# Adaptive-norm network of two layers on one core: the barrier between layer 0 and the attention is taken out and the first head starts among the last batch's experts

## The reference, cut to what matters

```python
# layer 0, for each batch: linear attention (16 heads of 8) + MLP on a modulated norm, then experts
h = _layernorm(x) * (1 + ca) + sa;  x = x + ga * L0_attn(h)
x = x + gb * L0_ffn(x modulated by cb, sb)
# layer 1, attention:
xn = layer_norm(_layernorm(x) * (1 + ca) + sa)
q, k, v = heads(xn @ Wq), heads(xn @ Wk), heads(xn @ Wv)
att = einsum('bhid,bhjd->bhij', q, k) / 8 + slope[h] * -|i - j|
p = softmax(att);  x = x + ga * ((p @ v) @ Wo)
```

## Time and profile before

| | |
|---|---|
| runs | 2463.85 us median of 3 (2462.29 to 2464.60) |
| profiled execution | 2467.89 us, span 2466.0 us |
| granted TensorE clock, mean | 0.954 of full |
| busy | PE 93%, DVE 71%, POOL 56%, ACT 52% |
| the chain that ended last | PE 86%, DVE 6%, issue 3%, POOL 2% |

### The profile page before, as it was taken

How to read it: one execution, slowest core, us unless ns; L and a number is a source line. 1 busy time by engine, 2 the same in 40 slices (tenths; PEclk the granted TensorE clock), 3 DMA queues, 4 the chain that set the end, 5 groups by cost and what they waited for, 6 DMA issues and landing times.

```text
span 2466.0 us, 39735 instructions
## 1 busy us (share of the span) xinstructions
PE 2296.2 (93%) x10653; PEld 1363.7 (55%) x10654; DVE 1740.9 (71%) x4461; ACT 1285.7 (52%) x1712; POOL 1385.0 (56%) x751
## 2 busy tenths in 40 slices
PE   4989898599999999999999999999999997969995
PEld 2566565356565655555555555555556553437663
DVE  5687785477777777777777777877787864744444
ACT  1223322266666666666666666666666662314442
POOL 2121120177676768676767777777767684743221
PEclk7999898599999999999999999999999997989998
DMA  7001202100000000000000000000000002111114
GB/s 266 1 6 74 80 1 79 31 14 10 15 11 13 18 15 11 13 12 13 21 11 12 13 14 10 13 20 14 10 15 11 13 20 113 38 39 45 43 42 126
DMA packets 71231, 81.41 MB, mean 33 GB/s; under 512 B 18324, under 2 KB 56980, under 8 KB 71000
## 3 DMA queue, kind: packets, MB, share of 16 engines
q1 hardware_dynamic: 66808, 71.58, 9.2%
q0 software_dynamic: 4352, 8.99, 1.1%
HBM read 49.97 MB, written 32.66 MB: 34 GB/s over the span
## 4 chain that ended last, share of the span: by engine, by line
PE 86%; DVE 6%; issue 3%; POOL 2%; SPq 1%; DMA 1%; ACT 1%; POOLq 0%; DVEq 0%; ACTq 0%
PE P L1774 18%; PE P L1738 12%; PE P L1759 9%; PE P L1760 9%; PE P L1725 5%; PE P L1596 3%; PE P L1969 3%; PE P L1973 3%; PE P L1610 3%; PE P L1992 3%; PE P L1781 2%; PE P L1792 2%; PE P L1707 2%; PE P L1743 1%; PE P L1982 1%
## 5 line engine op out<-in xcount | busy, mean ns | idle before, releaser
L1393 ACT ACTIVATE big<-P 128x1024 f32<-128x1024 f32 x512 | 511.9, 1020 | 188.4 <-PE P L1760 84.5
L998 DVE CUSTOM_DVE_ANT_0 big<-P,near 128x512 f32<-128x512 f32 x512 | 349.0, 682 | 231.4 <-PE P L1738 231.2
L1774 PE MATMUL P<-big,V 128*64 128x512 f32 x2048 | 481.3, 602 | 0.0
L601 POOL TENSOR_TENSOR spair<-spair,big 128x1024 f32<-128x1024 f32 x192 | 456.9, 2380 | 13.2
L601 POOL TENSOR_TENSOR opair<-opair,big 128x1024 f32<-128x1024 f32 x192 | 456.6, 2378 | 13.8 <-ACT big L1393 0.6
L1738 PE MATMUL P<-Ka,Qa 96*128 96x512 f32 x1024 | 451.8, 463 | 4.8 <-DVE mhalf L998 3.3
L1001 DVE TENSOR_REDUCE mhalf<-P 128x1 f32<-128x512 f32 x512 | 349.2, 682 | 85.9 <-PE P L1738 75.9
L1759 PE MATMUL P<-Qa,Ka 97*128 97x512 f32 x1024 | 408.4, 399 | 0.5 <-ACT big L1393 0.5
L1760 PE MATMUL P<-Qb,Kb 128*128 128x512 f32 x1024 | 406.5, 397 | 0.0
L1738 PEld LDWEIGHTS P<-Ka,Qa 96*128 96x128 f32 x1024 | 185.9, 191 | 224.4 <-issue 118.6
L588 POOL TENSOR_TENSOR big<-big,sinv 128x512 f32<-128x512 f32 x64 | 81.8, 1279 | 378.5 <-DVE sinv L973 378.5
(11 more groups left out here) (288 smaller groups left out, 3483.8 us busy)
## 6 DMA issues: line engine op xcount, KB each, us to landing
slots<-later SPq DMA_DIRECT2D x4, 4224.0 KB, 13.8
Ka<-auxrows SPq DMA_DIRECT2D x66, 128.0 KB, 2.2
big<-in_wex SPq DMA_DIRECT2D x8, 768.0 KB, 9.0
xt<-slots SPq DMA_DIRECT2D x76, 66.0 KB, 1.8
wqk<-in_whead SPq DMA_DIRECT2D x66, 64.0 KB, 1.8
near<-in_aux SPq DMA_DIRECT2D x66, 64.0 KB, 1.8
big<-yrows SPq DMA_DIRECT2D x8, 512.0 KB, 7.2
hT<-hkeep SPq DMA_DIRECT2D x5, 512.0 KB, 3.8
```

The source lines that it names most:

```text
L601: pool.tensor_tensor(psum8[s][:, :], psum8[s][:, :], pfull[:, j % RING, :], ALU.add).then_inc(S["p_added"], 1)
L998: dve.tensor_tensor_reduce(scratch, P[:, 6 + i, :], near[s][:, left:left + HALF], -1.0, 3.0e38, ALU.add, ALU.min, mhalf[:, i, t:t + 1]).th ...
L1393: act.activation(pfull[:, j, :], banks(2 * (j % 2)), ACT.Exp, scale=DH1 ** -0.5).then_inc(S["exp_done"], 1)
L1774: mm = pe.matmul(P[64 * i:64 * i + 64, 4, :], V1[:, j, s, :], half(pfull[:, j, :], i), start=(j == 0), stop=(j == T - 1))
```

## The change

The barrier between layer 0 and the attention is gone (`meet(8)` and one `end_batch` on each engine), and the code of both stages is in one semaphore epoch. The parts:

- SP issues the loads for heads 0 and 1 before layer 0. After `hkeep[2]` is written it waits until it has landed and loads `hTc` from `hkeep[0]`. After the last `up` of batch 3 it loads `hT` from `hkeep[0]`.
- In batch 3, PE projects q and k of head 0 from `hTc`, half 0 before the experts (`early_qk(0, 0, 6)`), half 1 after `down(2)`, and issues the maxima of head 0 in single matmuls after the downs of u = 5 to 17 (`early_max`). ACT and DVE split and reduce them among their GELUs and gates. Three maxima, head 1's projection and the turn follow the last `down`.
- The c part of batch 3 stands beside head 0's scores: `c_residual`, the moments, `c_first`, `c_second` and `c_third` (the three parts of `c_norms`) between DVE's biases. It uses `big[0]`, `big[1]` and `spair` as buffers. Its transposes come after `weigh(5)`.
- The maxima of head 1 no longer stand beside head 0's scores; they come after the c part's copies.
- Fillers: 3 or 2, and 2, before the two halves of the turn of `o0`; 6 for 2 before `turn("b0")` from batch 1 on; 4 new ones between its halves; 5 for 4 after it.
- `half_stats` of `c0`, half 1, moves ahead of DVE's wait for the exponential of q, in batches 1 to 3.

```diff
+            for b in range(B):          # SP
+                sp.dma_start(part, over(empty, [128, quarter, chunk])).then_inc(G["filled"], 16)
+                if b == B - 1:
+                    sp.wait_ge(S["up_mm"], EACH["up_mm"] * B)
+                    sp.dma_start(hT[:, :], hkeep[0]).then_inc(S["hT_in"], 16)
+                    sp.wait_ge(S["hT_in"], 32)
+                    sp.sem_inc(S["h_ok"], 2)
+                sp.wait_ge(E["c_kept"], NHALF * (b + 1))
+                sp.dma_start(hkeep[b], kept[b]).then_inc(G["h_kept"], 16)
+                if b == B - 2:
+                    sp.wait_ge(G["h_kept"], 16 * B)
+                    sp.dma_start(hTc, hkeep[0]).then_inc(S["hT_in"], 16)
             sp.wait_ge(G["h_kept"], 16 * B + 16)
...
+                if b > 0:               # DVE, between q0_min and the wait for q0_exp
+                    half_stats(f"c0{b - 1}", 1, tok(xs[:, b - 1, :]))
...
+                if b == B - 1:          # DVE, after the router
+                    q_low(0, 0, 0, 6)
+                    k_low(0, 0, 0, 6)
...
+                    elif u == 4:        # DVE, in the experts of batch 3
+                        q_low(0, 0, 1, 7)
+                        k_low(0, 0, 1, 7)
+                    elif u >= 6:
+                        early_max(u - 6)
+            for k in range(CH0 * NHALF - 6, T * NHALF):
+                early_max(k)
+            max_both(0)
+            c_residual(B - 1)
+            q_low(1, 1, 0)
+            k_low(1, 1, 0)
+            bias(0, 0, 0)
+            bias(0, 0, 1)
+            c_moments(B - 1, 0)
+            q_low(1, 1, 1)
+            k_low(1, 1, 1)
+            bias(0, 0, 2)
+            c_moments(B - 1, 1)
+            bias(0, 0, 3)
+            c_first(B - 1)
+            bias(0, 0, 4)
+            bias(0, 0, 5)
+            c_second(B - 1)
+            bias(0, 0, 6)
+            c_third(B - 1)
+            bias(0, 0, 7)
...
+                    if b == B - 1:      # ACT, in the experts of batch 3
+                        if u == 4:
+                            q_high(0, 0, 1, 7)
+                            k_high(0, 0, 1, 7)
+                        elif u == 8:
+                            q_again(0, 0)
+                        elif u == 10:
+                            k_again(0, 0)
...
+                if t == TPH and between:    # PE, turn
+                        keep_busy(4, between)
+                    keep_busy(4, 3 if i == 0 and b > 0 else 2)
-                keep_busy(2, 10 if b == 0 else 2)
+                keep_busy(2, 10 if b == 0 else 6)
-                turn(f"b0{b}", 2)
-                keep_busy(4, 4)
+                turn(f"b0{b}", 2, between=4)
+                keep_busy(4, 5)
...
+                if b == B - 1:          # PE, after zero(1)
+                    pe.wait_ge(E["c_kept"], NHALF * b)
+                    early_qk(0, 0, 6)
...
+            for k in range(EARLY, T * NHALF):   # PE, after close(1)
+                early_max(k)
+            early_qk(1, 0, 5)
+            turn_max(0)
+            pe.wait_ge(S["xb_done"], EACH["xb_done"] * B)
+            scores(0, 0, 0)
+            scores(0, 0, 1)
+            early_qk(1, 1, 5)
+            scores(0, 0, 2)
+            project_v(0, 0)
+            scores(0, 0, 3)
+            scores(0, 0, 4)
+            project_v(0, 1)
+            scores(0, 0, 5)
+            scores(0, 0, 6)
+            scores(0, 0, 7)
+            for j in range(T - 2):
+                weigh(0, 0, 0, j)
+            turn(f"c1{B - 1}", 6, xcs[B - 1])
+            pe.wait_ge(E["c_kept"], NHALF * B)
             for t in range(T):
                 for i in range(NHALF):
+                    max_half(1, 1, t, i)
+                if t == 1:
+                    project_qk(0, 2, 0)
+                if t == 4:
+                    project_qk(0, 2, 1)
+            weigh(0, 0, 0, T - 2)
+            weigh(0, 0, 0, T - 1)
+            turn_max(1)
```

More of the change, by code:

```diff
@@ L408, in _ @@
             sp.sem_inc(S["mod_in"], 1)
[L409 to L414, removed]
             def load_qk(g, s):
@@ L578, in _ @@
                     scale(b + 1, wdowns, wdown[:, :, :], 1, "wdown_scaled")
+            add_head(0, 0, False, range(1, 2))
             inverse_root(f"c0{B - 1}")
+            add_head(0, 0, False, range(2, 3))
             inverse_root(f"c1{B - 1}")
[L581 to L604, removed]
+            add_head(0, 0, False, range(3, T))
+            pool.wait_ge(G["h_kept"], 16 * B + 16)
+            add_head(1, 1)
             def first_pairs(b, behind):
@@ L1072, in _ @@
+            max_both(1)
             head(0, 1, behind=1)
@@ L1316, in c_copies @@
                     act.wait_ge(S["turned"], NHALF * TR_TAGS[f"c1{b}"] + i + 1)
-                    act.activation(half(hTc, i), P[:, 6 + i, :], ACT.Identity, bias=vecs[:, 5 + FC:6 + FC], scale=vecs[:, 4 + FC:5 + FC]).then_inc(E["c_kept"], 1)
+                    act.activation(half(kept[b], i), P[:, 6 + i, :], ACT.Identity, bias=vecs[:, 5 + FC:6 + FC], scale=vecs[:, 4 + FC:5 + FC]).then_inc(E["c_kept"], 1)
             act.wait_ge(G["set_done"], NSET)
@@ new lines, in _ @@
+            q_high(1, 1, 0)
+            k_high(1, 1, 0)
+            maxima(0, 0)
+            exps(0, 0)
+            exps(0, 1)
+            q_high(1, 1, 1)
+            k_high(1, 1, 1)
+            exps(0, 2)
+            exps(0, 3)
+            values(0, 0)
+            q_again(1, 1)
+            exps(0, 4)
+            values(0, 1)
+            exps(0, 5)
+            exps(0, 6)
+            exps(0, 7)
+            c_copies(B - 1)
+            q_high(0, 2, 0)
+            k_high(0, 2, 0)
@@ L1454, in _ @@
+            k_again(1, 1)
+            q_high(0, 2, 1)
+            k_high(0, 2, 1)
+            maxima(1, 1)
+            q_again(0, 2)
             head(0, 1, behind=1)
@@ new lines, in down @@
+            def down(b, u):
+                if u < NHALF:
+                    pe.wait_ge(S["up_act"], EACH["up_act"] * b + u + 1)
+                else:
+                    pe.wait_ge(S["up_gated"], EACH["up_gated"] * b + u - NHALF + 1)
+                f = A[:, (0 if u < NHALF else 2) + (u % 4) // 2, (u % 2) * HALF:(u % 2 + 1) * HALF]
+                for t in range(TPH):
+                    mm = pe.matmul(bank_t(0, u % 2 * TPH + t), tile(f, t), wdowns[:, u // NHALF, :],
+                                   start=False, stop=False)
+                mm.then_inc(S["downb_mm"], 1)
```

554 lines of the change are left out of this document (293 added, 261 removed).

## The result

The kernel after the change takes 2436.19 us, median of four runs (2431.65 to 2437.33), for 2464.22 (2462.29 to 2465.82) before: a ratio of 0.9884, 95% interval 0.9869 to 0.9899, so 28 us less where 33 were forecast. The time lies in the range. The profiled execution has 2437.33 us for 2467.89, which is 30.6 less; it is the slowest of its four runs.

What follows compares the result with a forecast made beforehand. TensorE bounds attention heads and experts; time lies at the boundary and in half-clock stretches. Boundary net 20.5, statistics 2.4, fillers 8.7 and 1.4 sum to 33.0 us saved: 2434.9 profiled, 2431 forecast, range 2420 to 2447.

Steps and rivals of the forecast that it cites:

- T0 to head 1's start, less what head 1 loses: Boundary, from the end of layer 0's experts (T0): 57 us for 83.7, half-clock loss in head 1 included, 26.8 saved.
- experts of batch 3 pay: Batch 3's experts: head 0's projections, splits and maxima placed there lose 6.3 us, bounds 5.4 and 15.
- fillers, both parts: Behind `b0`, full clock in three batches of four saves 8.7 us; in the attention part about 1.4.
- statistics: Batches 1 to 3: four DVE statistics of 0.79 us leave the chain, 2.4 us saved, lower bound zero.
- wait for `hTc`: Head 0's early projection in batch 3 waits for this load: taken as zero, 1 to 3 us if late.
- Rival E: Attention loop: loads run at another phase; 62 heads growing by 0.54 us each would eat the 33; slower, chance 0.04.
- F: Rival: no change, because the wait for `hTc` or for SP takes what the barrier gave; chance 0.02.
- B: Rival: fillers don't hold the clock, which stays near 0.5 at `b0`; 20 us saved, 2444 us, chance 0.22.
- D: Rival: head 0's weave is slower, biases behind c work, POOL's roots behind additions; 10 us more, 2441 us, chance 0.10.
- the 52 to 57: Sign in the profile after: head 1's first scores come 52 to 57 us after T0.
- "POOL's roots fall between its additions": Boundary, head 0: POOL's roots for the c part are ready before they are due.
- "That list doesn't run on TensorE's clock, so of this second part only 1.5 counts": Behind `b0`: DVE's router list limits the gates' turn, so ups and fillers gain only 1.5 us; 2.9 a batch in all.

Runs made afterwards that it cites:

- experiment 1: Changed kernel with the old fillers and the statistics at their old place, so the boundary alone: 2463.47 us for 2483.53, ratio 0.9917.
- experiment 2: Kernel before the change with the new fillers and nothing else: ratio 0.9951.
- experiment 7: Changed kernel with `half_stats` back in its old place: ratio 0.9897.
- experiment 10: Same kernel as experiment 9, but with layer 0's statistics at their old place: 2443.65 us, ratio 0.9837.
- experiment 4: Changed kernel with head 0's first projection in batch 3 behind `down(1)` and ACT's split behind its GELU of u = 2: ratio 0.9883.
- experiment 3: Changed kernel with POOL's additions of head 0 from block 2 on behind the c part's roots and DVE's last norm: 2448.67 us, ratio 0.9860.
- experiment 6: Changed kernel with blocks 6 and 7 of head 0 weighed around the c part's transposes, not behind head 1's maxima: ratio 0.9899.
- experiment 5: Changed kernel where SP loads head 2's `wqk` without waiting for the store of `hkeep[3]` to land: ratio 0.9885.
- experiment 8: Changed kernel with the four edits of experiments 3, 4, 5 and 6 together: ratio 0.9857.
- experiment 9: Kernel of experiment 8 plus fillers, eight before the wait for the c part and three behind each quarter of head 1's maxima: 2443.99 us, ratio 0.9834.

## Why the prediction was right, and where it was off

The sum had 33.0 us, and its own profiled execution shows 30.6. Term by term:

| term | forecast | measured |
|---|---|---|
| T0 to head 1's start, less what head 1 loses | 26.8 | 24.6, head 1 loses nothing |
| experts of batch 3 pay | 6.3 | 5.7 (experiment 1), 7.6 with new fillers |
| fillers, both parts | 10.1 | 12 to 15 (experiment 2) |
| statistics | 2.4 | 0 (traces of experiments 7, 10) |
| wait for `hTc` | 0, if late 1 to 3 | 2.6 with projection and split (experiment 4) |

The mechanism is the one forecast, but that the sum came so near is in part luck: the sum was too low by 2 to 5 us for the fillers and by 2.8 for head 1, and too high by 2.4 for the statistics, 5.2 for the way to head 1 and 1.3 for the experts.

*What bounds it.* Right: a head stayed at 24.46 us, units in batch 3 are 2.20 us and TensorE's, and the gain is all in the two places named. Rival E is out (no head has grown), F too, and B: the clock behind `b0` is held. Of D a part came true, 3.9 us for its 10, but not by POOL's roots.

*The boundary.* First scores come 5.4 us after T0, head 1's projection, biases and c part follow in the order laid out, and the wait for `wqk` is 2.85 for 3.3. Head 1 begins 59.2 us after T0, outside the 52 to 57 that were named as the sign. The step that failed is the c part taken at its old 13.12 us with waits for POOL's roots only. "POOL's roots fall between its additions" looked at POOL's list and not at what an addition does to DVE: 3 norms of 2.38 us, 4.7 us on the path (experiment 3). The last bias ends at T0 + 30.9 in the kernel after; without the long norms, in experiment 3, at T0 + 26, where 27 was forecast. The c part's copies end at T0 + 33.3 for 29.7. Behind them it is 25.9 us to head 1 for 24.3: the sum had all weighing hidden, and the last two blocks stood alone for 3.68 us, of which experiment 6 took 1.8 away. Against this another step erred the other way: head 1 was to begin at half clock (2.8 lost) and began at 0.95. From T0 it was 59.2 us for 54 + 2.8.

The Trainium skill has a rule that gives such a wait: in "SBUF — State Buffer", SBUF: two separate sides, the port pair that VectorE shares with GpSimd is an exclusive lock and no split of bandwidth, for a VectorE instruction in a two-port mode or with two SBUF inputs, and who starts first keeps it for the whole instruction. This trace agrees: a norm that begins behind an addition ends 0.08 to 0.09 us after it, 3 of 3 times, and 18 of 18 with experiments 1, 4, 5, 6 and 7. In which mode the norms run no view shows, so that they are of this kind is inferred from the match. The rule would have put a bound on this step, which the prediction did not look for: one addition's length for each addition that begins among the norms.

*The experts of batch 3.* From the logits' first matmul to the end of the last `down` it is 43.4 us before and 49.1 in experiment 1: 5.7 for the 6.3. With the new fillers the stage costs more, 7.6 us: 48.1 in the kernel after, 40.6 in experiment 2. In the kernel after the projection doesn't find TensorE waiting at half clock. It waits for `hTc` (0.73 us by itself in the kernel after), and ACT's split of q and k waits with it, ahead of the table load and the first GELU. The sum had no term for that split. Behind the wait the clock was 0.57, and two `up`s took 2.58 us for 1.7; but the wait alone doesn't bring the fall, since experiment 5 waited 0.92 us and kept 1.00. The prediction took zero for the wait; its "1 to 3" was right in size.

*Fillers.* The mechanism was right and its size too small. Four batches and not three held the clock behind `b0`, and batches 1 and 2 gained 4.1 us each (95.9 to 91.8) for 2.9 + 0.5. "That list doesn't run on TensorE's clock, so of this second part only 1.5 counts" was too careful. The chain of batch 2 shows what follows the logits:

```profile
278.49 1.08 PE P L1638 x5
279.57 1.83 PE P L1660 x16
...
282.40 1.28 ACT L1505
283.69 0.61 ACT big L1505
```

It goes by ACT's exponential, table load and first GELU, and not by the end of DVE's router. From the logits' end to the first `down` it is 2.9 us for 4.3 before, beside the logits' own 1.4 and 0.6 of the fillers.

*Statistics.* The 0.8 us a batch were there (experiments 5 and 7), but a clock fall at the MLP, 1.0 to 1.3 us in each batch, stood beside them. No step of the prediction looked for a fall in a stage that had 1.00 before.

*What remains.* By the timed ratios experiments 1 and 2 sum to 32.8 us and the whole change has 28 to 29; that difference is within the intervals. By the traces' last scores they have 18.9 and 15.4, 34.3 together, for 29.1. Of the 5.2 us between, 1.9 lie ahead of batch 3, where the MLP's falls stand, 2.3 in batch 3 (1.9 of them the experts' 7.6 for 5.7), and 1.0 behind T0, which was not traced.

## What to carry over

When a barrier falls and two stages share a stretch, list for each pair of engines what their instructions do to each other there, not only who waits for whom: GpSimd's long additions held VectorE's short norms. Fillers are worth a full clock on the chain behind them, but the clock is one resource along the whole line: four edits here, each of which shortened its own stretch by 1.8 to 4.7 us, sum to 11.1 and gave 8.0 at the attention's last scores (6.7 by the ratios). Of the missing 3.1, 1.9 went in head 1, which began before the clock was back. Judge an edit by marks behind the next full-clock stretch, not by its own.

## What the runs showed of the hardware beyond that

- A VectorE tensor_scalar of 128x128 fp32 in SBUF took 0.34 us, and 2.37 to 2.39 where it began just behind a GpSimd addition of 2.38 to 2.42 us: one norm for each of three additions. It is the same in experiments 1, 4, 5, 6 and 7: of these 18 norms each ended 0.08 to 0.09 us after its addition, and one that began 0.34 us behind it took 2.12. With the additions moved, 0.335 to 0.343 in all 16 (experiment 3).
- The granted clock at the same place of the same TensorE code differs between executions: 0.57 at the MLP of batch 1 of the kernel after, 1.00 in experiment 5; head 1 takes 22.3 us in four kernels (after, 1, 3 and 7) and 23.8 to 24.8 in experiments 4, 5, 6, 8, 9 and 10, by whether the clock is back when it begins.
- In the kernel after, TensorE worked 16.85 of 24 us (452 to 476) at a clock of 0.51, in pieces of 1 to 2 us with waits of 0.4 to 2.9 between; with fillers between them (experiment 9) it had 1.00.
